# Last layer of a four-layer transformer kernel: an order changed on ScalarE and GpSimd, one subtraction moved to GpSimd, one copy moved to ScalarE

## The reference, cut to what matters

```python
q = (query @ Wq + bq).reshape(B, S, N_HEADS, HEAD_DIM).transpose(0, 2, 1, 3)
k = (key @ Wk + bk).reshape(B, S, N_KV_HEADS, HEAD_DIM).transpose(0, 2, 1, 3)
v = (value @ Wv + bv).reshape(B, S, N_KV_HEADS, HEAD_DIM).transpose(0, 2, 1, 3)
...
scores = jnp.where(keep[None, None], scores, NEG)
probs = jax.nn.softmax(scores, axis=-1)
attn = jnp.matmul(probs, v)
attn = attn.transpose(0, 2, 1, 3).reshape(B, S, D)
attn = attn @ Wo + bo
gate = jax.nn.silu(jnp.concatenate([attn, query], axis=-1) @ Wg + bg)
out = attn * gate + query * (1.0 - gate)
x_hat = out * jax.lax.rsqrt(jnp.mean(out * out, axis=-1, keepdims=True) + EPS) * rms_w
return x_hat - jnp.mean(x_hat, axis=1, keepdims=True)
```

## Time and profile before

| what | value |
|---|---|
| median of 3 runs | 2344.29 us (2343.64 to 2345.33) |
| the profiled execution | 2352.8 us, its span 2351.0 us |
| TensorE busy (matmuls), share of the span | 2131.1 us, 91% |
| VectorE | 1514.2 us, 64% |
| ScalarE | 1086.2 us, 46% |
| GpSimd | 961.8 us, 41% |
| mean granted clock of TensorE | 0.980 |

### The profile page before, as it was taken

One profiled execution on the slowest core, in us unless ns is written; L12 is line 12 of the kernel. 1 busy time (PEld: TensorE's weight loads), 2 busy tenths in 40 slices (PEclk: granted clock), 3 DMA queues, 4 the chain that ended last, 5 costly groups with the idle time before them and its releaser, 6 DMA issues.

```text
span 2351.0 us, 81509 instructions
## 1 busy us (share of the span) xinstructions
PE 2131.1 (91%) x31188; PEld 1835.3 (78%) x31189; DVE 1514.2 (64%) x3179; ACT 1086.2 (46%) x2772; POOL 961.8 (41%) x1190
## 2 busy tenths in 40 slices
PE   5999999999999999999999939999999977888887
PEld 4878877878878778778778739999999965666665
DVE  4687787787787886887877851111111127999997
ACT  2354354454454453543543525555555534444444
POOL 3445455454554553654654531000000015656663
PEclk9999999999999999999999969999999999999999
DMA  8401001001001010010000044111111121111110
GB/s 201 152 3 39 10 18 41 11 19 35 16 19 31 20 32 13 20 37 8 21 21 6 19 143 142 36 36 36 38 36 36 36 61 47 57 47 54 56 52 18
DMA packets 93810, 101.00 MB, mean 43 GB/s; under 512 B 24304, under 2 KB 84720, under 8 KB 93424
## 3 DMA queue, kind: packets, MB, share of 16 engines
q1 hardware_dynamic: 83728, 69.93, 9.9%
q0 software_dynamic: 9440, 27.29, 3.6%
q10 hardware_dynamic: 384, 0.01, 0.0%
HBM read 64.95 MB, written 32.24 MB: 41 GB/s over the span
## 4 chain that ended last, share of the span: by engine, by line
PE 54%; issue 17%; DVE 14%; POOL 6%; ACT 5%; SPq 1%; DMA 1%; DVEq 1%; POOLq 0%; ACTq 0%
PE ps_scores L1049 11%; PE ps_w L1059 10%; PE ps_o L875 7%; PE ps_scores L836 4%; ACT pt_all L1202 4%; PE ps_qk L723 4%; PE ps_qk L757 3%; PE ps_xv L663 2%; DVE rs L1448 2%; PE ps_xv L741 2%; DVE lower L1429 2%; POOL lower L1857 2%; POOL rstd L1873 1%; PE ps_scores L783 1%; PE ps_scores L843 1%
## 5 line engine op out<-in xcount | busy, mean ns | idle before, releaser
L1441 DVE TENSOR_REDUCE mb<-ps_scores 128x16 bf16<-128x2048 f32 x160 | 365.8, 2286 | 43.8 <-PE ps_scores L816 39.8
L1956 POOL DMA_INDIRECT arena<-sorted_y,pidx x64 | 63.9, 998 | 609.1 <-ACT pidx L1313 584.4
L1448 DVE RECIPROCAL rs<-ps_o 128x256 f32<-128x256 f32 x160 | 280.4, 1753 | 31.3 <-PE ps_o L875 27.2
L1202 ACT ACTIVATE pt_all<-ps_scores 128x512 f32<-128x512 f32 x512 | 264.2, 603 | 65.2 <-PE ps_scores L843 63.4
L1049 PEld LDWEIGHTS ps_scores<-tiles,w_now 128*128 128x128 f32 x2272 | 266.1, 193 | 5.4 <-issue 1.8
L1049 PE MATMUL ps_scores<-tiles,w_now 128*128 128x128 f32 x2272 | 266.6, 276 | 1.2 <-DVE tiles L1717 1.2
L1287 ACT ACTIVATE tiles<-ps_scores,b1s 128x128 f32<-128x128 f32 x568 | 154.5, 383 | 238.4 <-PE ps_w L1059 230.9
L1059 PE MATMUL ps_w<-arena,tiles 128*128 x1136 | 257.0, 379 | 2.5 <-ACT tiles L1287 2.5
L1059 PEld LDWEIGHTS ps_w<-arena,tiles 128*128 128x128 f32 x1136 | 210.3, 190 | 28.6 <-issue 2.9
L1873 POOL TENSOR_TENSOR rstd<-ve,neghalf 128x1 f32<-128x1 f32 x192 | 109.9, 572 | 274.1 <-DVE ve L1459 266.3
L1857 POOL TENSOR_TENSOR lower<-lower,consts 128x512 fp32r<-128x512 f32 x160 | 171.3, 1070 | 117.9 <-DVE lower L1429 77.6
(11 more groups left out here) (233 smaller groups left out, 4531.5 us busy)
## 6 DMA issues: line engine op xcount, KB each, us to landing
tiles<-sorted_x SPq DMA_DIRECT2D x72, 128.0 KB, 2.0
sorted_y<-tiles SPq DMA_DIRECT2D x71, 128.0 KB, 1.7
w_experts<-in_L_xattn_e_w SPq DMA_DIRECT2D x6, 1024.0 KB, 11.7
arena<-in_L_xattn_e_w POOLq DMA_DIRECT2D x12, 384.0 KB, 4.1
ct_scratch<-cT SPq DMA_DIRECT2D x32, 128.0 KB, 1.7
x_scratch<-x2b_all SPq DMA_DIRECT2D x32, 128.0 KB, 1.8
arena<-x_scratch SPq DMA_DIRECT2D x32, 128.0 KB
cT<-ct_scratch SPq DMA_DIRECT2D x32, 128.0 KB, 2.1
```

What stands on the lines that cost most here:

```text
L1202: nc.scalar.activation(pt[:, 4 * g:4 * g + 4, :].rearrange("p h q -> p (h q)"), ps_s[:, g, :], ACT.Exp, bias=bias, scale=LAYER[l]["scale"] ...
L1441: V.tensor_reduce(mb[:].rearrange("p (g r) -> p g r", g=BANKS)[:, :, 0:SLOTS], ps_s[:].rearrange("p g (h k) -> p g h k", h=SLOTS), AX_X, A ...
L1448: V.reciprocal(rs[:], ps_o[:, 2:4, :]).then_inc(recip_ready, 1)
```

## The change: what it does

- ScalarE copies `atT` ahead of `mean_square`, and `index_prep` moves up behind `qk_evac(nxt)`.
- GpSimd's `gather(c(4))` moves ahead of `expand(nxt)`. `c_residual` is done one sequence earlier (`nxt` in place of `now`) and waits for `combine_apply(nn)` as well.
- The subtraction that makes `gd` (L1786) leaves VectorE; GpSimd does it in `difference(g_)` at the end of its step, and VectorE's second instruction of `gate_apply` waits for it. A sequence has 4 counts of `c_gstep` in place of 5.
- The copy of the values into `vz` leaves VectorE (two instructions, L1402); ScalarE does it in one, behind the tanh. It adds no bias. `bv` is multiplied with `Wo` once ahead of the loop and goes into `ln3_b_bo` and, through `bo3`, into the bias of the gate. For this the preparation has six more matmuls and two more additions; one load of `bv` along the rows goes, and a column joins `cols`.

```diff
@@ TensorE, ahead of the loop
+        for o in range(KC):
+            for c in range(KC):
+                mm(ps_o[:, 0, o:o + 1], w3o[:, c, P * o:P * (o + 1)], bv3, start=c == 0, stop=c == KC - 1)
         for c in range(KC):
-            last = mm(ps_w[:, 0:D], col["L3_xattn_bo"][:, c:c + 1].to_broadcast([P, P]), w3g[:, c, :], start=c == 0, stop=c == KC - 1)
+            last = mm(ps_qk[:, 0:D], bv3.to_broadcast([P, P]), w3o[:, c, :], start=c == 0, stop=c == KC - 1)
+        last.then_inc(c_bo_psum, 1)
+        pe.wait_ge(c_prep, 1)
+        for c in range(KC):
+            last = mm(ps_w[:, 0:D], bo3[:, c:c + 1].to_broadcast([P, P]), w3g[:, c, :], start=c == 0, stop=c == KC - 1)
         last.then_inc(c_bo_psum, 1)
@@ ScalarE
+        def vz_evac(n):
+            wait(act, v_psum, n["t"] + 1)
+            own = vz[n["p"]][:].rearrange("p h a b d -> p h (a b) d")[:, :, 0:4:3, :]
+            nc.scalar.copy(own, ps_xv[:, D:D + HD].unsqueeze(1).unsqueeze(1).to_broadcast([P, H // 2, 2, HD])).then_inc(vz_ready, 1)
@@ ScalarE, run_c
             if nxt["ok"]:
                 qk_evac(nxt)
-            if h_["ok"]:
-                mean_square(h_)
+            if c(4)["ok"]:
+                index_prep(c(4))
             if g_["ok"]:
                 wait(act, c_att_psum, g_["b"] + 1)
                 nc.scalar.copy(atT, ps_xv[:, 0:D].rearrange("p (c q) -> p c q", c=KC)).then_inc(c_att_sb, 1)
+            if h_["ok"]:
+                mean_square(h_)
             if now["ok"]:
                 mt_evac(now, True)
             if nn["ok"]:
                 xt_evac(nn)
-            if c(4)["ok"]:
-                index_prep(c(4))
...
+            if nxt["ok"]:
+                vz_evac(nxt)
@@ VectorE
+        V.tensor_tensor(bo3[:], col["L3_xattn_bo"], ps_o[:, 0, 0:KC], ALU.add).then_inc(c_prep, 1)
+        dve.wait_ge(b_y, TILES + 2)
+        V.tensor_tensor(ln3_b_bo, ln3_b_bo, ps_qk[:, 0:D], ALU.subtract).then_inc(c_prep, 1)
+        dve.wait_ge(c_bo_psum, 2)
...
             gate_link(n, 1, V.tensor_tensor(gu, ps_w[:, 0:D], row3["L3_xattn_bg"][:], ALU.add))
-            gate_link(n, 2, V.tensor_tensor(gd, at[n["s"]], xrb[n["s"]], ALU.subtract))
...
-            gate_link(n, 3, V.scalar_tensor_tensor(gu, ge, 1.0, gu, ALU.add, ALU.mult))
-            gate_link(n, 4, V.scalar_tensor_tensor(gd, gd, 0.5, gu, ALU.mult, ALU.mult))
+            gate_link(n, 2, V.scalar_tensor_tensor(gu, ge, 1.0, gu, ALU.add, ALU.mult))
+            wait(dve, c_diff, n["b"] + 1)
+            gate_link(n, 3, V.scalar_tensor_tensor(gd, gd, 0.5, gu, ALU.mult, ALU.mult))
@@ VectorE, run_c
             if g_["ok"]:
                 gate_open(g_)
-            if nxt["ok"]:
-                vz_evac(nxt)
             if c(3)["ok"]:
                 combine(c(3))
@@ GpSimd
+        def difference(n):
+            wait(pool, c_at, n["b"] + 1)
+            wait(pool, c_gstep, GATE * n["b"])
+            G.tensor_tensor(gd, at[n["s"]], xrb[n["s"]], ALU.subtract).then_inc(c_diff, 1)
@@ GpSimd, run_c
             if nn["ok"]:
                 c_root(nn)
+            if c(4)["ok"]:
+                gather(c(4))
             if nxt["ok"]:
                 expand(nxt)
             if h_["ok"]:
                 wait(pool, c_ve, h_["b"] + 1)
                 G.tensor_tensor(rstd[3][:], ve[3][:], neghalf[:], ALU.pow).then_inc(c_rms, 4)
-            if c(4)["ok"]:
-                gather(c(4))
-            if now["ok"]:
-                c_residual(now)
             if nxt["ok"]:
+                if nn["ok"]:
+                    wait(pool, c_ln, 6 * (nn["b"] + 1))
+                c_residual(nxt)
                 expand_lo(nxt)
+            if g_["ok"]:
+                difference(g_)
```

More of the change, by code:

```diff
@@ L55 @@
                  "L3_xattn_bq", "L3_xattn_bo"]
-COLS = len(COL_NAMES) * KC + FC + 1 + E * FC
+COLS = len(COL_NAMES) * KC + FC + 2 + E * FC
 def constants():
@@ L255, in program @@
     bff1, bk3 = cols_all[:, n_c:n_c + FC], cols_all[:, n_c + FC:n_c + FC + 1]
-    b1T = cols_all[:, n_c + FC + 1:COLS]
+    bv3 = cols_all[:, n_c + FC + 1:n_c + FC + 2]
+    b1T = cols_all[:, n_c + FC + 2:COLS]
     col = {n: cols_t[:, i, :] for i, n in enumerate(col_names)}
@@ L265, in program @@
             ("L3_xattn_bo", "L3_xattn_bg", "L3_xattn_rms_w", "L2_xattn_ln3_g", "L2_xattn_ln3_b")}
-    bv3 = sb("bv3", [HD])
+    bo3 = sb("bo3", [KC])
     rw, rb = sb("rw", [KC, E]), sb("rb", [E])
@@ L381, in program @@
     c_exp = sem("c_exp")
+    c_diff = sem("c_diff")
     c_prep = sem("c_prep")
@@ L470, in program @@
     RT2 = 6
-    GATE = 5
+    GATE = 4
     ROUTE_TAIL = 11
@@ L539, in late_loads @@
                     sp.dma_start(row3[n][:], a[n].rearrange("(o d) -> o d", o=1).partition_broadcast(P)).then_inc(ld_l3, 16)
-                sp.dma_start(bv3[:], a["L3_xattn_bv"].rearrange("(o d) -> o d", o=1).partition_broadcast(P)).then_inc(ld_l3, 16)
             if tau == 5:
@@ L1339, in run_c @@
                 qk_evac(now)
+                vz_evac(now)
                 xt_evac(nxt)
@@ L1398, in vz_evac @@
             wait(dve, v_psum, t + 1)
-            if l == 4:
-                src = ps_xv[:, D:D + HD]
-                for par in range(2):
-                    last = V.tensor_tensor(vz[p][:, :, par, par, :], src.unsqueeze(1).to_broadcast([P, H // 2, HD]),
-                                           bv3[:].unsqueeze(1).to_broadcast([P, H // 2, HD]), ALU.add)
-            else:
-                src = ps_xv[:, D:2 * D].rearrange("p (h two d) -> p h two d", two=2, d=HD)
-                bv = LAYER[l]["bv"]
-                for par in range(2):
-                    if bv is None:
-                        last = V.tensor_copy(vz[p][:, :, par, par, :], src[:, :, par, :])
-                    else:
-                        last = V.tensor_tensor(vz[p][:, :, par, par, :], src[:, :, par, :],
-                                               rows[bv].rearrange("p (h two d) -> p h two d", two=2, d=HD)[:, :, par, :], ALU.add)
+            src = ps_xv[:, D:2 * D].rearrange("p (h two d) -> p h two d", two=2, d=HD)
+            bv = LAYER[l]["bv"]
+            for par in range(2):
+                if bv is None:
+                    last = V.tensor_copy(vz[p][:, :, par, par, :], src[:, :, par, :])
+                else:
+                    last = V.tensor_tensor(vz[p][:, :, par, par, :], src[:, :, par, :],
+                                           rows[bv].rearrange("p (h two d) -> p h two d", two=2, d=HD)[:, :, par, :], ALU.add)
             last.then_inc(vz_ready, 1)
@@ L1740, in _ @@
         tile_y(TILES - 1, 0, (TILES - 1) // 2)
-        dve.wait_ge(ld_l3, 16 * 11)
+        dve.wait_ge(ld_l3, 16 * 10)
         V.tensor_copy(w3k[:], w3kv_raw[:, 0].unsqueeze(2).to_broadcast([P, KC, HPC, HD])).then_inc(b_y, 1)
@@ L1809, in run_c @@
                 qk_lo(now)
-                vz_evac(now)
                 combine(nn)
@@ L1969, in c_residual @@
             G.tensor_tensor(xr[n["s"]][:], xr[n["s"]][:], row3["L2_xattn_ln3_b"][:], ALU.add).then_inc(c_xr, 1)
+        def difference(n):
+            wait(pool, c_at, n["b"] + 1)
+            wait(pool, c_gstep, GATE * n["b"])
+            G.tensor_tensor(gd, at[n["s"]], xrb[n["s"]], ALU.subtract).then_inc(c_diff, 1)
         for par in range(2):
             pool.wait_ge(b_stored[par], 16 * ((TILES + 1 - par) // 2))
-        pool.wait_ge(ld_l3, 16 * 11)
+        pool.wait_ge(ld_l3, 16 * 10)
         def run_c(j, st, b, first, last):
             c = cparts(j, st, first, last)
-            now, h_, nxt, nn = c(0), c(-3), c(1), c(2)
+            now, g_, h_, nxt, nn = c(0), c(-2), c(-3), c(1), c(2)
             if first and st == 0:
@@ L1985, in run_c @@
                 expand(now)
+                c_residual(now)
                 expand_lo(now)
@@ L2032 @@
         [chunks(inputs[n]) for n in COL_NAMES] + [chunks(inputs["L0_xattn_b_ff1"])]
-        + [_np.tile(_np.asarray(inputs["L3_xattn_bk"]), HPC).reshape(P, 1)]
+        + [_np.tile(_np.asarray(inputs["L3_xattn_" + n]), HPC).reshape(P, 1) for n in ("bk", "bv")]
         + [_np.asarray(inputs["L2_xattn_e_b1"]).reshape(E * FC, P).T], axis=1)
```

6 lines of the change are left out of this document (3 added, 3 removed).

## The result

The changed kernel takes 2337.7 us in the median of 20 runs (2331.2 to 2343.7), where the kernel before, run beside it, took 2348.3 (2343.4 to 2352.6). The ratio is 0.9959, with a 95% interval of 0.9949 to 0.9968: faster by 0.4%, some 10 us, where the prediction had 45. The direction held, the size did not, and the time lies outside the forecast range.

The account below looks back on a forecast made before the run. VectorE was taken to pace the last layer's steps, 12.53 us falling to 10.8: 25 steps save 43.2 us, the ends 2.0, so 45 off 2344.3 gives 2299 us. Forecast range 2285 to 2314; wider range 2283 to 2318.

Parts of the forecast that it names:

- part (4): TensorE: early `atT` ends the 1.7 us wait ahead of L1090; 0.6 us idle stays ahead of L855, costing nothing.
- part (2): VectorE operations held by GpSimd's work: their excess time falls from 1.5 to 0.85 us a step.
- The layout: GpSimd's new order over one step from `maxima`: gather at 0.9 us, `expand` from 3.2, `difference` done at 9.4.
- part (1): VectorE loses L1786 and both L1402, 0.9 us a step, and the 0.14 us wait ahead of L1402.
- The covers (3): GpSimd's moved work stays hidden: `difference` has 0.4 us to spare, the root 0.6; GpSimd takes 9.6 of 10.8 us.
- rival A: GpSimd becomes the pace, step 11.8 us: 20 us off, 2324 us; chance 0.12.
- C: Gathers hold GpSimd longer, so VectorE waits for root and `difference`: step 12.8 us, 2349 us; chance 0.06.
- B: VectorE's contention with GpSimd goes altogether, TensorE paces at 10.2 us: 60 us off, 2284 us; chance 0.04.
- D: No change: one VectorE-GpSimd meeting swapped for another, a wait replaces what VectorE loses; 2344 us; chance 0.04.
- a sign of being wrong: Changed profile: VectorE's excess staying at 1.5 us, or VectorE idle for GpSimd over 0.3 us a step.
- The preparation (5): Ahead of the loop, four tiny matmuls and an addition make the first gather 2.1 us later.
- The 2.0 counted for the early step: Of the steps before the stretch, one, of 13.21 us, gains some 2.0 us.

Follow-up runs that it names:

- The added products: The changed kernel with two further, unused TensorE products of 128x256 in each `gate`, ahead of its own; ratio 0.9904 to the kernel before.

## Why the prediction went wrong

**The step that failed** is the end of part (4): TensorE's idle time, put ahead of the maxima's transposition by the early `atT`, was "costed at nothing more", with 0.6 us of it left and a clock at 2.4 GHz. TensorE's idle time is not its wait for one operand; as long as VectorE sets the step, it is step minus work, wherever it lies. Measured: 1.13 us a step ahead of L856, in lumps of 2.2 us and more in every second step, a clock of 0.93, and VectorE 0.29 us a step idle for scores. Before, the lower clock fell on the gate's products; now it falls on the scores, for which VectorE stands. The added products show that this costs time: without any other edit the kernel gets 0.5% faster, and with `qk_lo` first, where the clock is at 1.00 already, they bring nothing.

The edit itself decides less than that. Alone on the kernel before it costs 1%, by VectorE's wait for the values; in the changed kernel, taking it back changes little (0.9940 beside 0.9959) and, with `qk_lo` first, nothing that can be told (0.9859 beside 0.9867). What decides there is the order of `qk_lo` and `combine_apply`: with `qk_lo` first, L856 starts 3.2 us behind the start of `maxima` instead of 3.5 to 4.9, and a third of TensorE's waiting moves ahead of L664. That `combine_apply` is held is not needed for the loss: with the gather back it is free, and the wait ahead of L856 (1.20 us) and the clock (0.93) are as before. That the early copy "is what lets the rest count" did not hold: without it TensorE waited for 0.38 us a step, not 1.7.

**The collisions, part (2), were mis-sized,** and are the largest term. The excess was to fall by 0.65 us, from 1.5 to 0.85; it fell by 0.15, from 1.55 to 1.40. The layout missed one meeting. Its rule named operations with two SBUF inputs only, and it gave `combine_apply`, which reads one tensor, no cost; beside GpSimd's gather and `expand` it is held like the others, 0.95 us on average instead of 0.40. The reading of the rows was also a little off: a held operation does not do all its own work behind GpSimd's, as it ends 0.28 us behind it in the earlier trace rows, where it takes 0.42 by itself, and 0.15 us behind it in the step above. The Trainium skill (GPSIMD Engine Reference, section 8, Key points) names, besides VectorE instructions with two SBUF inputs, those in a 2-port performance mode. The trace shows that `combine_apply`, with one, meets contention (1.63 us in the step above); in which mode it ran no run here shows. The other meetings were foreseen: L1777, L1779 and L1815 above 0.5 us, the gate near 0.43.

**VectorE's own savings, part (1), came in part.** The three instructions took 0.82 us a step off VectorE's busy time, of the 0.9 forecast. The difference is worth 0.5% of the time, 0.47 us a step by the traces. But the values' copy, for which the forecast counted 0.47 us and the 0.14 of the wait, gave 0.26 alone (0.3%), for with it out of the way VectorE stands for 0.30 us ahead of L1777. That stand was not foreseen. Taking it away gained nothing clear.

**The sum.** Against 10.84 the step measured 11.91, 1.07 more: 0.50 less fall of the excess, 0.30 for the stand ahead of L1777, 0.29 for the wait for scores, 0.08 less off VectorE, 0.07 of waiting for the root. Less by 0.13, what VectorE had stood behind L1794 before (3.3 us in 25 steps), and by 0.06, its short idle times ahead of L1786 and L1402; 0.02 is rounding.

**What held.** The covers (3): no wait for the difference, 1.7 us in 24 steps for the root, and GpSimd busy for 8.4 us of 11.9, so rival A (it becomes the pace) did not come, nor C. B did not come either. D's first half, that one meeting is swapped for another, is much of what the excess shows, and that it stays near 1.5 was named as a sign of being wrong. The wait for `atT` went, as said. The preparation (5): the first gather starts at 1926.69, 2.3 us later when counted from the end of the last tile's work, forecast 2.1; yet the first `maxima` follows that end after 22.2 us against 22.1 before, so the loop's start absorbed it. The same 25 steps took 297.03 us (1978.36 to 2275.39) where they had taken 313.27: 16.2 less, of the 43.2 forecast. Of the remaining 1.3 us of the 17.5, 1.05 is that the last tile's work ended earlier (1921.35 against 1922.40), which the change has no part in; from there to the stretch it is 0.2 us longer, and behind the stretch 0.4 us shorter. The 2.0 counted for the early step did not come, nor did most of the 2.1 for the ends behind.

**What was not in any rival:** the place of TensorE's idle time. It was written down, priced at nothing, and never made a case of its own; the forecast gave 0.06 to slower ways and named for them only GpSimd. The gain that there is goes with the moved subtraction: without it the ratio is 1.0007, so the other parts together brought nothing. What stays open: what `qk_lo` first would give on the kernel before.

## What to carry to other kernels

When another engine paces, TensorE's idle time can't be removed, only placed: look at what stands behind it and who waits for that. Here two shorter gaps in a step went with a full clock, and one of 2.2 us ahead of the scores mostly did not. When work on GpSimd is moved, VectorE's operations with SBUF inputs pay at another place (1.00 to 1.60 us a step in the orders tried here); choose the one that pays by what is queued behind it, above all what TensorE waits for. Read several steps in a row, for a step can be good and the next one bad. And an edit whose price is "nothing, it is hidden" should be run alone on the kernel before, and taken back alone in the changed one: the two prices can differ, as they do here.
